# Input moments, two normalisations and the features of a state-space block: three stages and a small load made into one stage that works by halves

## The reference, cut to what matters

```python
def _layernorm(x, axis=-1, eps=1e-05):
    m = jnp.mean(x, axis=axis, keepdims=True)
    v = jnp.var(x, axis=axis, keepdims=True)
    return (x - m) / jnp.sqrt(v + eps)

def _L0_attn_ref(x, W_dt, b_dt, W_B, W_C, D_param, A_log, gamma, beta):
    residual = x
    mu = jnp.mean(x, axis=-1, keepdims=True)
    var = jnp.var(x, axis=-1, keepdims=True)
    xn = (x - mu) * jax.lax.rsqrt(var + LN_EPS) * gamma + beta
    dt = jax.nn.softplus(xn @ W_dt.T + b_dt)
    ...
    y = jnp.transpose(ys, (1, 0, 2)) + D_param * residual
    return y

h = _L0_tok_ref(...)                       # patches to tokens
h = jnp.concatenate([h, txt], axis=1)      # (16, 113, 256)
h = h + _L0_attn_ref(_layernorm(h, axis=-1), ...)
...                                        # seven more blocks
```

## Time and profile before

| what | value |
|---|---|
| runs | 1528.30, 1528.45, 1531.62 us, median 1528.45 us |
| profiled execution | 1516.85 us |
| its span (first to last instruction) | 1515.1 us |
| busy: PE, DVE, ACT, POOL | 1078.5, 1060.7, 708.5, 502.0 us |
| mean granted TensorE clock | 0.832 |

### The profile page before, as it was taken

One profiled execution on the slowest core, in us unless ns is written; L12 is line 12 of the kernel. 1 busy time (PEld: TensorE's weight loads), 2 busy tenths in 40 slices (PEclk: granted clock), 3 DMA queues, 4 the chain that ended last, 5 costly groups with the idle time before them and its releaser, 6 DMA issues. The chain is left out here.

```text
span 1515.1 us, 31541 instructions
## 1 busy us (share of the span) xinstructions
PE 1078.5 (71%) x9872; PEld 753.6 (50%) x9872; DVE 1060.7 (70%) x2352; ACT 708.5 (47%) x1416; POOL 502.0 (33%) x643
## 2 busy tenths in 40 slices
PE   4605887775279998687666968267579996479991
PEld 2202232223268886355444765144456664468881
DVE  3967999998735653765986863778858886735553
ACT  4505655564245553324435742144348886334440
POOL 0051677774055542751001100000026665232204
PEclk9557899997589999896977978678759997589996
DMA  6600000001065454422000000000013332112214
GB/s 203 219 3 11 1 1 0 1 1 37 13 172 137 130 165 129 128 69 83 2 1 1 1 1 0 0 1 0 0 61 100 113 114 68 49 51 65 64 51 121
DMA packets 47766, 89.68 MB, mean 59 GB/s; under 512 B 8352, under 2 KB 34629, under 8 KB 46789
## 3 DMA queue, kind: packets, MB, share of 16 engines
q1 hardware_dynamic: 40578, 67.98, 14.3%
q0 software_dynamic: 6912, 18.88, 4.3%
q10 hardware_dynamic: 144, 1.05, 0.2%
HBM read 71.84 MB, written 16.04 MB: 58 GB/s over the span
## 5 line engine op out<-in xcount | busy, mean ns | idle before, releaser
L1039 POOL TENSOR_TENSOR scan_ch<-scan_hs,scan_ct 128x452 f32<-128x452 f32 x128 | 143.3, 1141 | 81.5 <-DVE scan_hs L1149 68.1
L1062 PE MATMUL scan_py<-scan_ch,ident 128*128 128x452 f32 x256 | 130.9, 600 | 41.0 <-POOL scan_ch L1039 31.1
L1149 DVE TENSOR_TENSOR_SCAN scan_hs<-scan_abar,scan_bx 128x452 f32<-128x452 f32 x128 | 132.9, 1079 | 0.8 <-ACT scan_abar L1111 0.5
L458 PE MATMUL m0x_ph<-m0x_xb,m_w_hi 128*128 128x128 f16 x456 | 99.2, 219 | 0.2
L459 PE MATMUL m0x_ph<-m0x_xb,m_w_hi 128*128 128x128 f16 x456 | 99.2, 219 | 0.0
L460 PE MATMUL m0x_ph<-m0x_xb,m_w_lo 128*128 128x128 f16 x456 | 98.7, 218 | 0.0
L1876 DVE TENSOR_SCALAR m3x_a<-m3x_ph,m3x_b 128x128 f32<-128x128 f32 x184 | 49.7, 343 | 69.0 <-ACT m3x_ah L1837 69.0
L1062 PEld LDWEIGHTS scan_py<-scan_ch,ident 128*128 128x128 f32 x256 | 40.6, 193 | 112.4 <-POOL scan_ch L1039 104.2
L1111 ACT ACTIVATE scan_abar<-ssm_dt,ssm_a 128x448 f32<-128x448 f32 x128 | 80.8, 638 | 23.8 <-DVE scan_hs L1149 22.1
L1873 DVE SCALAR_TENSOR_TENSOR m0x_a<-m0x_ph,m0x_b,m0x_gate 128x128 f32<-128x128 f32 x114 | 34.7, 346 | 70.9 <-ACT m0x_gate L1821 68.8
L1837 ACT ACTIVATE m3x_ah<-m3x_ph,m3x_b 128x128 f16<-128x128 f32 x184 | 50.1, 383 | 64.5 <-PE m3x_ph L460 60.4
(11 more groups left out here) (692 smaller groups left out, 3833.0 us busy)
## 6 DMA issues: line engine op xcount, KB each, us to landing
mha_wbuf<-m3w SPq DMA_DIRECT2D x32, 512.0 KB, 3.3
tok_wbuf<-m0w SPq DMA_DIRECT2D x15, 768.0 KB, 4.4
m0x_b<-m0b SPq DMA_DIRECT2D x57, 128.0 KB, 3.4
m_out<-m0x_yo SPq DMA_DIRECT2D x57, 128.0 KB
m3x_b<-m3b SPq DMA_DIRECT2D x23, 128.0 KB, 3.2
m_out<-m3x_yo SPq DMA_DIRECT2D x23, 128.0 KB, 1.7
m_rows<-m0r_parts SPq DMA_DIRECT2D x4, 448.0 KB
m_rows<-m3r_parts SPq DMA_DIRECT2D x4, 448.0 KB
```

Source lines behind the costliest of these rows:

```text
L458: pe.matmul(out, w_hi, x_hi, start=start, stop=False)
L1039: pool.tensor_tensor(ch[r][:], hs[r][:], ct[n % 2][:], ALU.mult).then_inc(weighed, 1)
L1062: pe.matmul(py[c][:, 0:GT], core.ident[:], ch[u % R][:], start=n == 0, stop=n == NS - 1).then_inc(summed, 1)
L1149: dve.tensor_tensor_scan(hs[u % R][:], abar[c][:, 0:GT], bx[u % R][:], 0.0, ALU.mult, ALU.add).then_inc(scanned, 1)
```

## The change

One stage, `stage_norm_twice_features` (tag `f0`), takes the place of the load, the statistics, `twice` and the features. A class `Skip` holds the skip term's buffers, which now live through `stage_ssm_inputs` too.

- SP issues three transfers, gain, offset and `D_param`, all on one semaphore; ACT waits for all three (`landed`, 48) ahead of its first root, and POOL ahead of its products.
- DVE takes the statistics of `h` only. From one variance ACT takes two roots per half, of the norm that `core.xn` needs (`sd1`) and of both norms together (`sd2`). DVE makes two reciprocals and two shifts of them.
- The rows for the transposes come straight from `h` with `r2` and `shift2`: 6 batches by ACT, 10 by DVE. `core.xn` is written by ACT (`once`), 16 batches.
- Of a group's full values DVE writes one half of the channels and ACT the other.
- POOL waits until both halves' shifts are there and adds the skip term for batches 0 to 7; the other half of the pairs is appended to POOL's list in `stage_ssm_inputs`, behind the cast.

```diff
+    def add(self, pool, multiplied, added, pairs, n, ready):
+        b = slice(pairs[n] * (GB // 2), (pairs[n] + 1) * (GB // 2))
+        if ready is not None:
+            pool.wait_ge(ready, b.stop)
+        need(pool, added, n - 1)
+        pool.tensor_tensor(self.prod[n % 2][:], self.core.xn[:, b, :], self.row, ALU.mult).then_inc(multiplied, 1)
+        pool.wait_ge(multiplied, n + 1)
+        pool.tensor_tensor(self.core.h[:, b, :], self.core.h[:, b, :], self.prod[n % 2][:], ALU.add).then_inc(added, 1)
...
+    BY_SCALAR = (0, 2, 4, 8, 9, 12)
...
+                sp.dma_start(skip.skip[:], d["d_param"].partition_broadcast(L)).then_inc(landed, 16)
...
+                pool.wait_ge(landed, 48)
+                pool.wait_ge(by_scalar, sum(b < HB for b in BY_SCALAR))
+                pool.wait_ge(by_vector, sum(b < HB for b in BY_VECTOR))
+                pool.wait_ge(shift_ready, 2)
+                for n in range(HB // 2):
+                    skip.add(pool, multiplied, added, range(HB // 2), n, xn_ready)
...
+                def deviations(half):
+                    bs = slice(half * HB, (half + 1) * HB)
+                    act.wait_ge(var_ready, half + 1)
+                    act.activation(sd2[:, bs], var[:, bs], ACT.Sqrt, bias=eps2[0:L, :],
+                                   scale=(1.0 + EPS) / D).then_inc(sd_ready, 1)
+                    act.activation(sd1[:, bs], var[:, bs], ACT.Sqrt, bias=core.eps[0:L, :],
+                                   scale=1.0 / D).then_inc(sd_ready, 1)
...
+                act.wait_ge(landed, 48)
+                deviations(0)
...
+                def low(g):
+                    cols = slice(g * GT, (g + 1) * GT)
+                    dve.wait_ge(hi_done, g * KC + 1)
+                    dve.tensor_scalar(full[:, 0, cols], tp[g % 2][0][:, 0:GT], gam[:, 0:1], bet[:, 0:1], ALU.mult,
+                                      ALU.add).then_inc(full0_done, 1)
+                    for c, done in enumerate((full0_done, full1_done)):
+                        dve.wait_ge(done, g + 1)
+                        dve.tensor_tensor(core.xt_lo[:, c, cols], full[:, c, cols], core.xt_hi[:, c, cols],
+                                          ALU.subtract).then_inc(lo_done, 1)
...
+                stats(range(0, HB))
+                spread(0)
+                stats(range(HB, HB + 3))
+                scales(0)
+                for b in (1, 3):
+                    normalise(b)
+                stats(range(HB + 3, NB))
+                for b in (5, 6, 7):
+                    normalise(b)
+                spread(1)
+                low(0)
+                scales(1)
+                for b in (10, 11):
+                    normalise(b)
+                low(1)
+                for b in (13, 14, 15):
+                    normalise(b)
+                low(2)
+                low(3)
...
@@ stage_ssm_inputs, on POOL @@
+                for n in range(NB // 4):
+                    skip.add(pool, multiplied, added, range(NB // 4, NB // 2), n, None)
...
@@ block_attention0 @@
-            stage_load(nc, "gb", [(gam[:], d["gamma"]), (bet[:], d["beta"])])
-            stage_norm_stats(nc, core, "st0", core.h)
-            stage_norm_twice(nc, core, d["d_param"])
-            stage_features(nc, core, "f0", core.xn, affine=(gam, bet), full=ssm.dx)
-        stage_ssm_inputs(nc, core, d, ssm)
+            stage_norm_twice_features(nc, core, d, skip, gam, bet, ssm.dx)
+            stage_ssm_inputs(nc, core, d, ssm, skip)
```

More of the change, by code:

```diff
@@ L815, in _, with __init__ @@
                 low(3)
-def stage_norm_twice(nc, core, d_row):
-    with Stage(nc, "twice") as st:
-        skip = st.sb("skip", [L, D])
-        six = st.sb("six", [L, NB, 6])
[L824 to L828, removed]
+class Skip:
+    def __init__(self, core, skip, prod):
+        self.core, self.skip, self.prod = core, skip, prod
+        self.row = skip[:].unsqueeze(1).to_broadcast([L, GB // 2, D])
+    def add(self, pool, multiplied, added, pairs, n, ready):
[6 more added lines that the diff above has]
+        pool.tensor_tensor(self.core.h[:, b, :], self.core.h[:, b, :], self.prod[n % 2][:], ALU.add).then_inc(added, 1)
@@ new lines, in stage_norm_twice_features, with wait_place @@
+def stage_norm_twice_features(nc, core, d, skip, gam, bet, full):
+    BY_SCALAR = (0, 2, 4, 8, 9, 12)
+    BY_VECTOR = tuple(b for b in range(NB) if b not in BY_SCALAR)
+    HB = NB // 2
+    with Stage(nc, "f0") as st:
+        six = st.sb("six", [L, NB, 6])
+        total, diff, var, sd1, sd2, r2, shift1, shift2 = (
+            st.sb(n, [L, NB]) for n in ("total", "diff", "var", "sd1", "sd2", "r2", "shift1", "shift2"))
+        eps2 = st.sb("eps2", [128, 1])
+        xr = [st.sb(f"xr{u}", [L, GB, D]) for u in range(2)]
+        tp = [[st.ps(f"tp{u}{c}", [128, 512]) for c in range(KC)] for u in range(2)]
+        landed, eps_set = st.sem("landed"), st.sem("eps_set")
+        counted, moments, var_ready, sd_ready, recips, shift_ready = (
+            st.sem(n) for n in ("counted", "moments", "var_ready", "sd_ready", "recips", "shift_ready"))
+        by_scalar, by_vector, xn_ready = st.sem("by_scalar"), st.sem("by_vector"), st.sem("xn_ready")
+        tp_ready, hi_done, full0_done, full1_done, lo_done = (
+            st.sem(n) for n in ("tp_ready", "hi_done", "full0_done", "full1_done", "lo_done"))
+        multiplied, added = st.sem("multiplied"), st.sem("added")
+        def wait_place(eng, b):
+            eng.wait_ge(shift_ready, b // HB + 1)
+            need(eng, tp_ready, (b // GB - 1) * KC)
@@ L843, in _, with stats @@
[L843 to L865, removed]
+                def stats(blocks):
+                    for b in blocks:
+                        dve.bn_stats(six[:, b, :], core.h[:, b, :]).then_inc(counted, 1)
@@ new lines, in spread, with scales @@
+                def spread(half):
+                    bs = slice(half * HB, (half + 1) * HB)
+                    dve.wait_ge(counted, (half + 1) * HB)
+                    norm_moments(dve, Chain(dve, moments, half * 3), six[:, bs, :], total[:, bs], diff[:, bs], var[:, bs],
+                                 core.mean[:, bs], var_ready)
+                def scales(half):
+                    bs = slice(half * HB, (half + 1) * HB)
+                    dve.wait_ge(sd_ready, half * 2 + 2)
+                    dve.reciprocal(r2[:, bs], sd2[:, bs]).then_inc(recips, 1)
+                    dve.reciprocal(core.rstd[:, bs], sd1[:, bs]).then_inc(recips, 1)
+                    dve.wait_ge(recips, half * 2 + 2)
+                    dve.scalar_tensor_tensor(shift1[:, bs], core.mean[:, bs], -1.0, core.rstd[:, bs], ALU.mult, ALU.mult)
+                    dve.scalar_tensor_tensor(shift2[:, bs], core.mean[:, bs], -1.0, r2[:, bs], ALU.mult,
+                                             ALU.mult).then_inc(shift_ready, 1)
```

78 lines of the change are left out of this document (69 added, 9 removed).

## The result

The changed kernel took 1504.85 us (median of 4 runs, 1503.78 to 1507.30) against 1528.38 us (4 runs, 1525.34 to 1531.62) for the kernel before: ratio 0.9849, 95% interval 0.9832 to 0.9867, or 20 to 26 us less. The forecast was 1511.2 us, in a range of 1503 to 1518.5. Direction and range held; the gain was 23.5 us where 17.2 were forecast. The profiled execution took 1503.98 us, span 1502.2.

The account below looks back on a forecast made before the run. It took barrier-separated stages from load to features, with GpSimd finishing `twice` last, to add whole to kernel time: -22.4 (new stage) + 5.2 (`ssmin`) = -17.2 us, so 1528.45 - 17.2 = 1511.2 us, range 1503 to 1518.5.

Parts of the forecast that it names:

- The new wait: New stage: ScalarE's first root waits 3.7 us for the third transfer, the row, to land at 76.05.
- steps 1 and 2: New stage: VectorE starts at about 68.6 with work removed; moments at about 72.3, row landing 6.64 us after issue.
- Steps 3 and 5: New stage: roots, reciprocals and shifts, normalising from 77.2; VectorE's second scales at 84.1, only then GpSimd starts.
- Step 4: New stage: ScalarE's list of operations takes 20.1 us from 77.2, ending at 97.3 if it never waits.
- Step 6: New stage: VectorE's 7.7 us plus 10.1 held by GpSimd, less some 1.6, ends at 100.3; part -22.4 us.
- `ssmin`, +5.2: `ssmin`: five one-element operations each held for one GpSimd operation, delaying ScalarE's first operation 5.2 us; bounds 1.3 and 10.3.
- the first rival: `ssmin`: one-element operations are free, two or three `dt` and `dx` held; -22.4 + 2.9, 1509.0 us, chance 0.22.
- the second (1504.3): Both stages: VectorE hardly held, ScalarE's list alone sets the new stage, `ssmin` loses 1.3; -24.1, 1504.3 us, chance 0.10.
- the last sign of error: Behind the scan: a stage differing by over 2 us would show the forecast wrong.
- every GpSimd operation at its whole length: Both stages: every GpSimd operation costs its whole length; -20.2 + 10.3 = -9.9, 1518.5 us, chance 0.10.
- a later row: New stage: row lands later than 76.05, so the change only moves the wait; 1520 to 1528 us, chance 0.05.
- the clock in the experts: Experts: TensorE work left at the lower clock makes the kernel slower; 1536 us with 25 us left, chance 0.03.

Follow-up runs that it names:

- e_row: Changed kernel with the D_param row on its own semaphore, for which GpSimd alone waits, not ScalarE: 1501.85 us, ratio 0.9826.
- e_nof0: Changed kernel without the skip term of batches 0 to 7, GpSimd's four pairs in the new stage: 1502.12 us, ratio 0.982.
- a0: The changed kernel run and profiled again, no edit: 1507.03 us, ratio 0.9849.
- b0: The kernel before run and profiled again, no edit: 1526.87 us, ratio 0.9981 to its own companion runs.
- e_b_nostats: The kernel before without the second statistics, the second moments being constants: 1529.06 us, ratio 1.0001.
- e_warm: Changed kernel with 22 more matmuls ahead of TensorE's wait in `ssmin`: 1505.61 us, ratio 0.9857.

## Why the prediction was right, and where it was not

Direction and range were right, and the mechanism of the new stage was: three barriers and GpSimd's long list gone, a wait for the row, VectorE held. One step of `ssmin` was wrong. By the forecast's own numbers, then. The embedding ended at 70.24 in the changed kernel's profile and at 68.27 in the one before, so 1.97 us are taken off its stamps here. Two figures of the working stand in none of its rows: a pitch of 0.47 us between issues (the rows give 0.39 and 0.43) and 0.37 us for a row by VectorE (2.67 / 8 = 0.33). They move its sum by 0.5 us at most.

1. **The new wait** (steps 1 and 2): forecast 3.7 us, measured 3.5. The transfer took 6.38 us from issue to the root where 6.64 was taken from the earlier trace rows. e_row shows it on the path: 3.2 us.
2. **Steps 3 and 5**: normalising began at 79.05 - 1.97 = 77.1, forecast 77.2; GpSimd's first product at 85.82 - 1.97 = 83.9, forecast 84.1.
3. **Step 4**, ScalarE's list of 20.1 us: it ran from 79.05 to 99.45, 1.51 of it waiting; without GpSimd (e_nof0) 18.7. A little too long by the forecast.
4. **Step 6**, VectorE's holds: forecast 8.5 us (10.1 - 1.6), measured 6.4. The mechanism was right, the term too large: VectorE ended at 99.56 - 1.97 = 97.6, forecast 100.3. The whole part is -24.9 (55.1 to 30.2), forecast -22.4. This is a mis-sized term: operations that read PSUM, and waits that fall beside GpSimd's work, took off 3.7 us, not 1.6. Nor did the whole of the 6.4 us count: without them the stage is only 2.0 us shorter (e_nof0), as ScalarE's list then ends it. The stage's end at 97.6 is outside the 99 to 102 that the forecast gave as its sign.
5. **`ssmin`**, +5.2: measured +5.1 in one profile and +3.0 in the other, and **this is the step that failed**: "If held, each takes one GpSimd operation". No one-element operation is held: 0.15 us each, in every kernel run, beside GpSimd and without it. ScalarE's first `az` came 9.44 us after the stage's first transfer (100.05 to 109.49), where it was 8.29 before (122.99 to 131.28): 1.15 us later and not 5.2. The forecast had listed just this as a sign of being wrong. The nearest row, 16 elements at 1.17 us, was not near enough. What costs time in its place: the split, +1.1 (as forecast); two `dt`, +1.5 (forecast 1.65 if not held, so +2.9 in all, the rival's sum; a0 gives 3.0); and in the first profile TensorE's clock, which rose 6.0 us after the first matmul instead of 3.3 (before, and a0) and fell again at about 119.8 after an idle of 2.5 us. That the sum came out right in the first profile, by another cause, was luck.

The Trainium skill's rule that was weighed (VectorE: DVE Perf Modes, What auto-detection actually checks: a one-source operation goes through both ports if source and destination are in SBUF and their outermost non-unit dimensions are even or equal) agrees with the rows of 16 and of 256 elements, 1.17 us and 1.69 for two. With one element no dimension is left that isn't a unit; reading that as "equal" was mine, and the rows at 106.82 to 107.55 say that it is wrong.

6. **The sum.** To the scan the traces show -19.8 (before to changed) and -22.2 (b0 to a0), forecast -17.2; the timed ratio gives -23.5, its interval reaching to -20. About 2.5 us of the miss is the new stage, 2.2 the one-element operations where the clock rises in time. The likeliest case was not the one that came true; it was the first rival (one-element operations are free) with a better new stage. In time it lies near the second (1504.3), but only by its number: that one had VectorE hardly held.
7. **The base**, and the last sign of error, "a stage behind the scan that differs by over 2 us". Two do. The stretch from `mhaf` to the next routing is 192.0 us before and 188.6 changed, but 190.0 in a0, and 188.5 to 192.1 over all profiles, so this is scatter. And `shared` is 88.1 us in the profile before, 95.4 in the changed one. But it is 103.8 in b0, whose code is the same as before's, and over all thirteen profiles it goes from 88.1 to 103.8 (mean of the three of unchanged or nearly unchanged code before 97.1, of the ten others 98.1). So nothing shows it to be the change's. The 11.6 us between the profiled execution of before and its runs' median most likely lie there: that execution had the shortest `shared` of all, and b0, whose `shared` is 15.7 us longer, has a span longer by 17.9 (1533.0). Comparing the two spans alone (1515.1 - 1502.2 = 12.9 us) would have undersold the change by half. Adding the change to the median, as the forecast did, was the right choice.

The rivals: every GpSimd operation at its whole length (-9.9) falls with item 4; VectorE hardly held falls with its 6.4 us; a later row with item 1; the clock in the experts (1536 us) with the lengths behind the scan, where between the scan and `shared` no stage of the changed kernel is over 2 us longer than before (the nearest, the routing, has 65.4 against 63.4) and the window from 535 to 565 us, again in the experts, has a granted clock of 1.00 as in the earlier trace rows. e_b_nostats shows that the change's cheapest-looking part, 5.3 us of statistics, gave nothing alone.

## What to carry to other kernels

Before removing VectorE work from a stage, look which engine ends last: here 10 us of it (21.71 against 11.25 us of waiting in e_b_nostats) left no mark until the work behind was let in beside GpSimd's list. GpSimd's elementwise work was not free beside VectorE operations between SBUF tensors (3.97 us for 1.05) and was free beside ones that read PSUM (0.73 us for 0.74, and a scan of 205.8 us with 19 us more of it), so the place to try first is beside a scan or other work that reads PSUM, in a step where GpSimd has idle time for a piece of its size. A semaphore shared by a small and a large transfer makes everybody wait for the large one (3.2 us here), and a term whose only row is sixteen times larger deserves both ends with equal weight.

## What the runs showed of the hardware that was not expected

- One-element VectorE operations (tensor with scalar, cast, int32 and fp32) take 0.14 to 0.16 us in the middle of a GpSimd operation on two SBUF tensors; 16 elements took 1.17 us, and the split of 256 columns 1.48 instead of 0.41.
- TensorE's clock can stay at its lower level (0.50, matmuls of 0.58 us) for 6.0 us after work begins in one execution and 3.3 in another of the same kernel (a0: 110.40 after 107.13); over the thirteen profiles, without e_warm, it is 2.7 (b0) to 6.0. It can fall back after idle times of 2.49 us (changed) or 3.93 (e_warm), while one of 2.71 at the same place in a0 and one of 3.08 in e_row left it at 1.00. The idle time of the engine alone does not tell which.
- `shared` scatters by up to 15.7 us between executions. In b0 VectorE's sum of 0.42 us starts 10.8 us after the last matmul ahead of it and TensorE stands with it, while GpSimd goes on issuing gathers:

```profile
645.22 0.27 PE L2057 MATMUL shared_po<-shared_b_lo,ones 1*113 1x256 f16 x1
```
```profile
653.07 0.95 POOL L1958 DMA_INDIRECT shared_got<-m_out,m_slot  x1 [0.30 <-issue]
```
```profile
656.29 0.42 DVE L2107 SCALAR_TENSOR_TENSOR h<-shared_po,h 113x256 f32<-113x256 f32 x1 [14.03 <-remote]
```

  The profile of before has no wait marked "remote" in that stage; a0 has 30.0 us of them before ScalarE's `shared_gate`. What the engines wait for there stays open; no run was made for it, as it isn't the change's.
